# Graph network, four layers on one core: 23 extra row gathers in the set-up, and bounds checks on values loaded for waits

## The reference

```
h = relu(layernorm(x)); x = x + GCN(h)      # three rounds: z = relu(segment_sum((z@W)[src] * norm, dst) + b)
h = relu(layernorm(x)); x = x + GIN(h)      # relu((h + segment_sum(ew*h[src], dst))@W1 + b1)@W2 + b2
h = relu(layernorm(x)); x = x + ATT(h)      # segment softmax over each node's edges, 8 heads, att = distance**lam
h = relu(layernorm(x)); x = x + SAGE(h)     # mean of neighbours @ W_l.T + b_l + h @ W_r.T, rows normalised
```

## Time and profile before

| | |
|---|---|
| time, median of 3 runs | 6554.8 us (6554.49, 6554.8, 6564.94) |
| span of the profiled execution, first to last instruction | 6553.3 us |
| busy, share of that span | PE 60%, DVE 48%, ACT 17%, POOL 72% |
| chain that ended last | POOL 56%, issue 20%, PE 12%, DVE 8% |
| first gather of pass 0 | at 193.57 us |

### The profile page before, as it was taken

How to read it: one execution, slowest core, us unless ns; L and a number is a source line. 1 busy time by engine, 2 the same in 40 slices (tenths; PEclk the granted TensorE clock), 3 DMA queues, 4 the chain that set the end, 5 groups by cost and what they waited for, 6 DMA issues and landing times.

```text
span 6553.3 us, 78540 instructions
## 1 busy us (share of the span) xinstructions
PE 3920.5 (60%) x20158; PEld 2753.8 (42%) x20158; DVE 3125.0 (48%) x8266; ACT 1109.3 (17%) x2896; POOL 4742.9 (72%) x4806
## 2 busy tenths in 40 slices
PE   1555555555555555555455555689999984555556
PEld 1333333433333433333333333556666663333344
DVE  7433333433333433333533333479999997223234
ACT  1000000000000000000100000268887873000001
POOL 7777777777777677777677777577777754777775
PEclk7656566666666756656565666799999996556657
DMA  2222122212122221222212112167776751222222
GB/s 59 79 53 53 52 53 53 72 53 53 53 53 53 66 53 52 53 53 53 63 53 52 53 53 52 50 150 155 155 154 153 154 123 36 53 53 53 53 53 56
DMA packets 384775, 465.36 MB, mean 71 GB/s; under 512 B 103806, under 2 KB 290636, under 8 KB 384348
## 3 DMA queue, kind: packets, MB, share of 16 engines
q0 software_dynamic: 152528, 313.83, 18.7%
q1 hardware_dynamic: 200958, 128.87, 8.8%
q10 hardware_dynamic: 30878, 17.63, 1.0%
HBM read 434.52 MB, written 27.81 MB: 71 GB/s over the span
## 4 chain that ended last, share of the span: by engine, by line
POOL 56%; issue 20%; PE 12%; DVE 8%; DMA 2%; SPq 1%; ACT 1%; DVEq 0%; ACTq 0%; POOLq 0%
POOL pool L791 55%; PE psum L1045 2%; PE psum L1021 2%; PE psum L1003 2%; PE psum L1010 2%; PE psum L933 1%; DVE work L1841 1%; PE psum L996 1%; PE psum L988 1%; DMA pool<-table,src_col 1%; PE psum L967 1%; DVE pool L1776 1%; DVE pool L1774 1%; PE psum L1033 1%; PE psum L920 1%
## 5 line engine op out<-in xcount | busy, mean ns | idle before, releaser
L791 POOL DMA_INDIRECT pool<-table,src_col x3910 | 3740.9, 957 | 1263.9 <-issue 1172.5
L967 PE MATMUL psum<-pool 128*128 x8300 | 1847.4, 392 | 2259.6 <-SPq L564 1860.7
L967 PEld LDWEIGHTS psum<-pool 128*128 128x128 f32 x8300 | 1600.8, 281 | 2770.9 <-issue 2762.6
L1725 DVE TENSOR_TENSOR work<-work,psum 128x1024 f32 x520 | 634.7, 1221 | 3155.4 <-PE psum L973 3154.3
L1735 DVE TENSOR_SCALAR pool<-iota_f,rel_col,ew_col 128x128 f32<-128x128 f32 x3320 | 890.0, 353 | 9.4 <-ACT work L1110 5.5
L763 POOL DMA_INDIRECT gath<-table,src_col x520 | 514.8, 990 | 174.7 <-issue 143.2
L973 PE MATMUL psum<-zero_rows,iota_b 128*128 128x512 bf16 x1040 | 521.4, 602 | 0.0
L958 PE MATMUL psum<-zero_rows,iota_b 128*128 128x512 bf16 x1040 | 493.5, 573 | 11.9 <-DVE work L1725 9.0
L1228 ACT ACTIVATE pool<-psum 128x512 f32<-128x512 f32 (+1 forms) x104 | 55.7, 562 | 1993.4 <-PE psum L920 1991.9
L763 POOL DMA_INDIRECT ew_col<-table,src_col x312 | 303.2, 972 | 95.2 <-issue 94.3
L1228 ACT ACTIVATE pool<-psum,gcn_bias 128x512 f32<-128x512 f32 (+1 forms) x26 | 17.1, 658 | 1950.5 <-PE psum L920 1950.3
(11 more groups left out here) (234 smaller groups left out, 3918.8 us busy)
## 6 DMA issues: line engine op xcount, KB each, us to landing
pool<-table,src_col POOLq DMA_INDIRECT x3910, 2.5
pool<-edge_attr SPq DMA_DIRECT2D x832, 64.0 KB
pool<-step_masks SPq DMA_DIRECT2D x624, 48.0 KB
pool<-rel_rows SPq DMA_DIRECT2D x208, 128.0 KB
table<-work ACTq DMA_DIRECT2D x48, 256.0 KB, 2.3
gath<-table,src_col POOLq DMA_INDIRECT x520
ew_col<-table,src_col POOLq DMA_INDIRECT x312
table<-QV SPq DMA_DIRECT2D x12, 256.0 KB, 2.3
```

The costliest lines, as they stand in the source:

```text
L791: gp.indirect_dma_start(out=gath_ring[:, t % RING, :], out_offset=None, in_=source[:, :], in_offset=bass.IndirectOffsetOnAxis(ap=src_col[: ...
L967: pe.matmul(window_sums(w)[:, bass.ds(places[s % REGS], 1), :].rearrange("p a d -> p (a d)"), hot_ring[:, s % HOT_RING, :], gath_ring[:, b ...
L1725: v.tensor_tensor(into, into, window_sums(a), ALU.add).then_inc(steps.added, 1)
```

## The change

There are two parts. In the set-up GpSimd numbers the 128 partitions (`row_no`) and, after the first piece of the powers, issues 23 further indirect DMAs that read rows of x by these numbers: 22 of 2 to 128 rows of 512 bytes into an end of `pool` that is used only later, and one of 128 rows of 1 KB. Nothing reads what they bring. VectorE waits for all 23 before it takes the step rows. In the second part the values that TensorE and ScalarE load for waits (batch numbers, window numbers) go through `load_waits`, which leaves the check of the bounds in.

```diff
--- before.py
+++ after.py
@@ -365,6 +365,12 @@
         masks_made = sem("masks_made")
         masks_stored = sem("masks_stored")
         pow_made = sem("pow_made")
+        rows_tried = sem("rows_tried")
+        row_no = sb("row_no", [P, 1], I32)
+        row_no_made = sem("row_no_made")
+        TRIED = (128, 127, 126, 125, 124, 123, 122, 121, 120, 119, 112, 100, 96, 64, 48, 32, 16, 8, 2, 128, 125, 124)
+        tried_rows = pool[:, NX - (len(TRIED) + 2) * D:NX].rearrange("p (k d) -> p k d", d=D)
+        assert at + 3 * NT <= NX - (len(TRIED) + 2) * D and E > 0
         pow_stored = sem("pow_stored")
         att_tiled = sem("att_tiled")
         att_rows_here = sem("att_rows_here")
@@ -522,6 +528,11 @@
                 plan_reg[which:which + 1, first:first + n:step], engines=[kind], min_val=least, max_val=top,
                 skip_runtime_bounds_check_because=reason)[1]
 
+        def load_waits(kind, which, first, n, top, step):
+
+            return nc.values_load_multi_w_load_instructions(
+                plan_reg[which:which + 1, first:first + n:step], engines=[kind], min_val=1, max_val=top)[1]
+
         def load_blocks(kind, first, n):
             return load_plan(kind, 0, first, n, NB - 1, "the plan takes the smaller of the block and the last block")
 
@@ -529,7 +540,7 @@
 
         def load_batches(kind, first):
 
-            return load_plan(kind, 3, first, REGS - BATCH + 1, ceil_div(NT, BATCH), "the plan takes one more than the batch of a tile", BATCH, 1)
+            return load_waits(kind, 3, first, REGS - BATCH + 1, ceil_div(NT, BATCH), BATCH)
 
         def load_bases(first):
             return load_plan(mybir.EngineType.DVE, 5, first * WINDOW, min(REGS, NW - first) * WINDOW, NB - WINDOW,
@@ -543,8 +554,7 @@
                 if j % REGS == 0:
                     n = min(REGS, last - j)
                     first = BATCH * j + BATCH - 1
-                    past = load_plan(mybir.EngineType.Activation, PLAN, first, (n - 1) * BATCH + 1, NW,
-                                     "a tile's last step is one of PS", BATCH, 1)
+                    past = load_waits(mybir.EngineType.Activation, PLAN, first, (n - 1) * BATCH + 1, NW, BATCH)
                 act.wait_ge(steps.done, past[j % REGS])
                 act.sem_inc(slots_free, 1)
 
@@ -721,9 +731,19 @@
                                      channel_multiplier=mult).then_inc(head_sum_made, 1)
                 n += 1
 
+            gp.iota(row_no[:, :], pattern=[[0, 1]], base=0, channel_multiplier=1).then_inc(row_no_made, 1)
             gp.wait_ge(lam_made, 1)
             gp.tensor_tensor(dist_sb[:, 0:FIRST_POW], dist_sb[:, 0:FIRST_POW], lam_row[:, 0:FIRST_POW],
                              ALU.pow).then_inc(pow_made, 1)
+            gp.wait_ge(row_no_made, 1)
+            for k, n in enumerate(TRIED):
+                gp.indirect_dma_start(
+                    out=tried_rows[0:n, k, :], out_offset=None, in_=x_in[:, :],
+                    in_offset=bass.IndirectOffsetOnAxis(ap=row_no[0:n, :], axis=0)).then_inc(rows_tried, 16)
+            pair = tried_rows[:, len(TRIED):len(TRIED) + 2, :].rearrange("p k d -> p (k d)")
+            gp.indirect_dma_start(
+                out=pair, out_offset=None, in_=x_in.rearrange("(n a) d -> n (a d)", a=2),
+                in_offset=bass.IndirectOffsetOnAxis(ap=row_no[:, :], axis=0)).then_inc(rows_tried, 16)
             gp.wait_ge(tile_idx_made, 1)
             gp.wait_ge(tiles_written, TILES_WRITTEN)
             for i in range(SR):
@@ -1337,6 +1357,7 @@
 
             plan_vector(v, own, settle)
             norm_x_vector(v, own, settle)
+            v.wait_ge(rows_tried, 16 * (len(TRIED) + 1))
             step_rows_vector(v, own, settle)
             degrees_vector(v, own, settle)
```

## The result

The changed kernel takes 6533.9 us (median of 4 runs, 6532.58 to 6541.48), the kernel before 6558.9 us beside it (4 runs). The ratio is 0.9961, 95% interval 0.9948 to 0.9973: faster by 0.39%. I had forecast 6555.6 us, with a range of 6551 to 6566 us, and no change that can be told, and given "faster" a chance of 0.03. The prediction was wrong.

What follows compares the result with a forecast made beforehand. GpSimd's gathers were taken to pace each pass, at about 1.26 us a gather. Set-up gathers 0 plus checks 0.8 us on the 6553.3 us span gave 6554.1 us of span, 6555.6 us of time, range 6551 to 6566 us.

Steps and rivals of the forecast that it cites:

- Nothing on the path starts earlier by the edit, so the lower bound is 0: Set-up: the added gathers cannot shorten the path; their cost is 0, with bounds 0 and +10.2 us.
- again at 0.957 + 0.30 us: Passes: each L791 gather keeps its 0.957 us and 0.30 us gap, with no wait for slots.
- The iota: Set-up on GpSimd: one short instruction while it waits for the distances, cost 0.
- The one on the faster side: Rival: a later second power makes a phase at a pass end fall better; 6540 us at most, chance 0.03.
- New gathers: Set-up gap on GpSimd: 23 at 0.957 + 0.26 + 0.30 us take 34.9 us, ending at 61.0 us; path cost 0.
- the bound of 1.82: Set-up: upper price per new gather, 1.82 us, ending at 74.9 us and costing +10.2 us.
- VectorE beside the gathers: Set-up: VectorE's plan work loses nothing beside gathers, 1.08 us an operation either way; only the gathers get dearer.
- Row gathers late: Rival, set-up: new gathers at 1.82 us or more delay row gathers beyond 5.0 us slack; +10.2 us, 6565 us; chance 0.07.
- Checks: Register instructions behind TensorE and ScalarE value loads: 74 ns each, 0.59 us per TensorE load, 2.4 us per ScalarE load.
- my 0.8 us: Total forecast cost of the bounds checks, from TensorE's loads at the ends of the five passes.
- The pass ends: TensorE's load at step 816: checks cost 0 in passes 0 to 2, 0.17 us in pass 3, 0.59 in pass 4.
- The rival of dear checks: Rival, TensorE's queue: each check costs as much as a TENSOR_LOAD, 1.105 us; +81 us, 6636 us; chance 0.05.

Runs made afterwards that it cites:

- e9: Kernel before plus the bounds checks and only the int32 iota with its room, no new gathers: 6534.5 us, ratio 0.9967.
- e10: Kernel before plus the bounds checks and only the SBUF room for `row_no` and its semaphore, no new GpSimd instruction: 6559.0 us, ratio 1.0018.
- e11: Kernel before plus the bounds checks and an iota with float32 output in place of int32, no new gathers: 6560.2 us, ratio 1.0006.
- e2: The changed kernel with all 22 gathers of x at 128 rows and the gather of 1 KB rows left out: 6532.6 us, ratio 0.9964.
- e8: Kernel before plus the bounds checks and one product and one sum on GpSimd between second power and pass 0, no new gathers: 6530.6 us, ratio 0.9964.
- e12: Kernel before plus the bounds checks and one 128-row gather in the set-up gap, its index from a memset, not the iota: 6558.7 us, ratio 1.0003.
- e13: The whole change, all 23 gathers and checks, with the index column from a memset in place of the int32 iota: 6575.6 us, ratio 1.0012.
- e5: The changed kernel with only one new gather, of 128 rows, in the gap behind the first power; checks kept: 6532.0 us, ratio 0.9965.
- e6: The changed kernel with only one new 128-row gather, behind the seven row gathers and ahead of the second power: 6534.1 us, ratio 0.9966.
- e7: The changed kernel with only one new 128-row gather in the gap, carrying the row gathers' bounds check: 6531.8 us, ratio 0.9961.
- e4: Kernel before plus the bounds checks and a GpSimd product and sum in the gap before the row gathers, no gathers or iota: 6556.3 us, 1.0002.

## Why the prediction was wrong

- **The step that failed** is "Nothing on the path starts earlier by the edit, so the lower bound is 0", with the gathers of the passes "again at 0.957 + 0.30 us". I took L791's mean as a constant of the instruction, though the sum hangs on it 3910 times: 1 ns is 3.9 us. In before it has two levels, 951/955 and 940/944 ns, and which holds depends on what GpSimd ran before (e9 against e10 and e11). With passes 0 to 3 at the level that before shows in pass 4, they would have taken 4 x 978.5 = 3914.0 us in place of 3947.7, 34 us less; 24.5 us came. The median fell by 10 ns, but the mean of these 3128 gathers only by 7.9: 261 of them take 970 ns or more in after, 175 in before.
- **The iota**, "one short instruction while GpSimd waits for the distances, 0": right for its own time (0.14 us, 4.37 us into the run), wrong in what it does to the others. No rival named it. The one on the faster side gave a later second power as the mechanism; e9 has the whole gain without it (its row gathers start at 59.1 us, those of before at 59.6).
- **New gathers**, 34.9 us to 61.0 us: they took 36.4 us for 22 and 1.26 us for the pair, to 63.75 us. Their mean of 1.349 us (22 gathers) against my 1.217 is inside the bound of 1.82. With 128 rows in each it was 32.9 us, so 3.5 us are the row counts, about half of them (2.98 - 1.28 = 1.7) the first odd one. The rest of the excess is there with 128 rows too, beside VectorE's plan, as the forecast had it.
- **VectorE beside the gathers**, "I price the plan's own work, which is on the path, at no loss": wrong. The earlier trace rows showed gathers of 128 rows. Beside one of 127 rows a VectorE operation stood still 1.75 us. Beside those of 125 and 124 rows two more did, 0.36 and 0.49 us, while with 128 rows in all of them (e2) no hold passes 0.24 us. The set-up loss is 4.1 us, of it 2.3 us from VectorE and most of the rest from TensorE's lower clock at the first dense product, which e8 shows without any new gather. The Trainium skill, "GPSIMD Engine Reference", section "Key points", says that GpSimd shares its SBUF interfaces with VectorE and names contention with two kinds of VectorE instructions, but not which engine loses. My prediction took it to be GpSimd alone; this case's trace shows VectorE held as well, 2.30 us against 0.55.
- **Row gathers late**: 4.4 us, inside the 5.0 us of slack, and of no cost. The mechanism of that rival was right in kind, but it didn't reach the path.
- **Checks**, 74 ns an instruction, 0.59 us a load on TensorE: measured 148 and 18 ns, 0.166 us a value and 0.66 us a load, so right in sum. On ScalarE 16 x 0.166 = 2.7 us a load against 2.4. With the checks alone the time is 1.0005 (0.9995 to 1.0015), +3 us at the middle, with my 0.8 us inside. The pass ends can't be told one by one: the 0.79 us of issue at the end of pass 4 is not on the chain of after, and the gaps between passes vary by up to 4 us between runs. The rival of dear checks falls. The 108 ns that the Trainium skill, "Advanced Engine Details and Errata", section "Control Flow Timing", gives for a compare-and-branch lies between the two kinds; my estimate from it was 0.86 us a load, against 0.66 measured.

**What stays open.** How GpSimd's history sets the time of a gather. The runs exclude as the source of the gain the room that `row_no` takes (e10), one more instruction ahead (e11) and further gathers (one in e12, 23 in e13). e5, e6 and e7 have the iota ahead, so they say nothing of their gather. What is left is a state that depends on which kinds of instruction GpSimd has run and in which order; at least three levels exist (944 and 955 ns in one trace, before, and 952 and 955 ns in one trace, e4). The Trainium skill, "GPSIMD Engine Reference", section "Instruction dispatch", says that GpSimd's cores run each instruction as a piece of software found by its opcode. That such code could lie more or less well after another order of first use is contradicted by none of the runs, but no run here shows it; it is an idea and not a finding.

## What to carry over

Where one instruction is repeated thousands of times on the path, look at the minimum and median of its duration stage by stage before you take it as a constant. Two levels in one trace say that something sets it, and then even an edit beside the path can move the whole sum. If a change brings a gain that its described mechanism can't give, take out its parts one by one, down to the shortest instruction, and the cause may be what carried no price. Look also at whether the engine is on the path in that stage: the same shorter gathers gave nothing in the attention stage. Here one iota with the checks does as well as the whole change: e9 has a ratio of 0.9967 and the change 0.9961, which the intervals don't tell apart. I wouldn't rely on the effect in another kernel without its trace.

## What the hardware showed that I had not expected

- The duration of GpSimd's indirect gathers of 128 rows goes by the earlier history of GpSimd: 944, 952 or 955 ns median, with the minimum moving along. From start to start a gather of passes 0 to 3 takes 1.254 us in e9 and 1.264 us in e10 on average, 7 us a pass of 782. A further shift of 3 ns comes and goes between profiles (947 and 958 ns) and isn't explained.
- The first gather with a row count other than 128 took 2.98 us (2.76 alone, 3.30 in e13), and the VectorE operation beside it took 1.33 to 1.75 us longer. Why only the first is so dear stays open.
- A bounds check on a loaded value is two queue instructions of 148 and 18 ns on TensorE and 147 and 18 ns on ScalarE.
